# The opening of a fused transformer kernel's first stage: who clears and rotates the keys, and where the modulation products run

## The chip, the cores and the metric

One core of a Trainium2 chip runs the whole program. The metric is the device time of one execution in microseconds (us).

## The reference

Two adaptive-layernorm transformer layers over an input of 4 sequences x 512 tokens x 256 features, float32. Only the first layer's attention and the modulation vectors matter here.

```
mod = silu(c) @ wmod                 # per layer: 6 vectors of 256 for each sequence
h   = layernorm(x) * (1 + scale) + shift
q, k, v = h @ wq, h @ wk, h @ wv     # in float16; 16 query heads, 4 key groups, 16 numbers a head
q, k = rope(rmsnorm(q)), rope(rmsnorm(k))
x   = x + gate * (causal_softmax(q k^T) v @ wo)      # then a small gated feed-forward
```

The second layer is a lightning attention with a mixture of experts behind it. It needs its own modulation vectors, and 16 decay masks (one for each head), which the first stage makes and stores to memory.

## The kernel before

The program has three stages with a barrier behind each: `front_stage` (the first layer), `attention1_stage` and `experts_stage`. The change touches the first alone.

`front_order` writes out one list of events, and each engine walks through that list in order and executes the events that belong to it. TensorE (PE) works on a ring of four PSUM slots of two banks: the m-th event of the ring may start only when event m-4 has been read out. So a late reader blocks PE, and a PE event that is early in the list holds up all behind it.

Work goes by sequence b (4) and by key group g (4), 16 groups in all. For each group the events `s` (eight, by token tile and pair of heads) make the scores whose row maxima VectorE takes (L930); at the last one VectorE writes the shift into the queries (L934), `q2` turns the shifted queries, `st` makes the transposed scores, ScalarE takes their exponential (L779), GpSimd masks them (L1079), and `pv` multiplies by v. The scores of group g+1 are interleaved with the `st` of group g.

The opening, ahead of group 0, is written out by hand:

- `L stats`, `L rstd`, `L norm`: statistics of the tokens on VectorE (L174, L177), the root on GpSimd (L184 to L191), the normalization on ScalarE (L198); `xt` turns the result on PE (L206) and ScalarE applies shift and scale from `mod` (L212).
- `mod`: the modulation products, four events (L580); `mod copy` (VectorE, L852 to L843) copies them out, adds 1 to the scales (L857), and after events 1 and 3 prepares the gates.
- `pj`: q, k and v of two token tiles each on PE (L602, L604), copied out by ScalarE (L749). `sq`, `ss`, `std`, `rms`, `qn` are the RMS norm: square (L513), sum (L887), root (L757, ScalarE, which needs another activation table than the exponential), reciprocal (L890), product (L898).
- `rot`, `rope`: all 16 query heads rotated on VectorE (L907 to L921). `krot`: the 4 key heads on GpSimd (L1062 to L1073).
- `kt`: the keys turned on PE (L610) and copied out (L765); SyncE (SP) then issues 16 DMAs (L552), four for each group, that spread them over the cleared buffer `kt`. GpSimd clears that buffer (L1037) after its root of `L rstd`; VectorE clears the query buffer `qa` (L871) after `L stats`.
- `qt`: the queries of one group turned (L621) and copied out (L768).
- `dec`: one decay mask each: exponential on ScalarE (L703), triangle mask on GpSimd (L1017), store by SP (L542).

SP issues the loads of all four `x` blocks and all weights first, then walks the list too.

Of the kernel before, what the change touches and what calls it, by code (L numbers as in the profile page):

```python
# [6 lines left out]
F32 = mybir.dt.float32  # L7
# [93 lines left out]
def front_order():  # L101
# [281 lines left out]
def front_stage(nc, t, d):  # L383
# [9 lines left out]
    x, hp = t["x"], t["h_parts"]  # L393
    NH, hd, SLOTS = H0 + G0, D0 // 2, 4
    with ExitStack() as ctx:
        n = Names(nc, ctx, "front")
# [53 lines left out]
        diag = hp[:, :, :, (B - 1) * S:B * S]  # L450
        wmod1 = (qt2[:, :, :].rearrange("p g n -> p (g n)").bitcast(F32).rearrange("p (k n) -> p k n", k=KT),
                 upd[:, :, :].rearrange("p t n -> p (t n)").rearrange("p (k n) -> p k n", k=KT), ht[:, :, :])
# [28 lines left out]
        a_high, a_low, b_high, b_low = (n.sem(s) for s in ("a_high", "a_low", "b_high", "b_low"))  # L481
        carried = n.sem("carried")
        gbias_ready, x_biased, ff_done, x_done = (n.sem(s) for s in ("gbias_ready", "x_biased", "ff_done", "x_done"))
# [19 lines left out]
        MODS = ((0, (0, 1)), (0, (2, 3, 4, 5)), (1, (0, 1, 2)), (1, (3, 4, 5)))  # L503

        def rows(b):
            return slice(b * TB, (b + 1) * TB)

# [7 lines left out]
        with nc.Block() as block:  # L515

            @block.sync
            def _(sp):
# [14 lines left out]
                sp.dma_start(wo32, d["wo0"]).then_inc(wo_loaded, 16)  # L533
                for b in (2, 3):
                    sp.dma_start(x[:, rows(b), :], d["x"][:, rows(b), :]).then_inc(x_loaded[b], 16)
# [25 lines left out]
            def _(pe):  # L561
                for ev in order:
# [49 lines left out]
                    elif kind in ("qt", "q2"):  # L612
                        o = banks16(ev)
                        if kind == "qt":
                            b, g = ev[1], ev[2]
                            pe.wait_ge(q_roped, b + 1)
# [75 lines left out]
            def _(act):  # L692
# [4 lines left out]
                for ev in order:  # L697
# [45 lines left out]
                    elif kind == "pj":  # L743
                        _, b, i = ev
                        filled(act, ev)
                        if b:
                            act.wait_ge(v_copied, b)
                            act.wait_ge(qn_done, b)
                        nc.scalar.copy(qkv[:, 2 * i:2 * i + 2, :], banks(ev)[:, :, 0:QKV0]).then_inc(qkv_done, 1)  # L749
# [58 lines left out]
            def _(dve):  # L808
# [7 lines left out]
                dve.wait_ge(cond_step, 2)  # L816
                nc.vector.tensor_tensor(scond[:, :, :, :], cond[:, :, :, :], scond[:, :, :, :], ALU.mult).then_inc(scond_ready, 1)
                dve.wait_ge(slope_loaded, 16)
                nc.vector.tensor_scalar(nslope[:, :], nslope[:, :], -1.0, None, ALU.mult).then_inc(slope_neg, 1)
                gates = 0  # L820

                def gate_then(ins):
                    nonlocal gates
                    gates += 1
                    ins.then_inc(gate_step, 1)
                    dve.wait_ge(gate_step, gates)

                def columns(l):
# [17 lines left out]
                for ev in order:  # L846
# [20 lines left out]
                    elif kind == "L stats":  # L867
                        dve.wait_ge(x_loaded[ev[1]], 16)
                        norm_l.vector_stats(nc, dve, ev[1])
                        if ev[1] == 0:  # L870
                            nc.vector.memset(qa[:, :, :, :, :].rearrange("p a t h c -> p (a t h c)").bitcast(F32), 0.0  # L871
                                             ).then_inc(padding_set, 1)
                    elif kind == "A stats":
# [5 lines left out]
                    elif ev == ("sq", 0):  # L879
                        dve.wait_ge(qkv_done, 2)  # L880
                        squares(nc.vector)
                    elif kind == "ss":
                        b = ev[1]
                        dve.wait_ge(sq_done, b + 1)
                        if b:
                            dve.wait_ge(qn_done, b)
                        nc.vector.tensor_reduce(ss[:, :, :], sq[:, :, :, :], AX.X, ALU.add).then_inc(ss_done, 1)  # L887
# [3 lines left out]
                    elif kind == "qn":  # L891
                        b = ev[1]
                        dve.wait_ge(rrms_done, b + 1)
                        if b:
                            dve.wait_ge(krot_done, 2 * b)
                        else:
                            dve.wait_ge(qkv_done, 2)
                        nc.vector.tensor_tensor(qn[:, :, :, :].rearrange("p t h c -> p (t h) c"),  # L898
                                                qkv[:, :, 0:NH * D0].rearrange("p t (h c) -> p t h c", c=D0),
                                                ss[:, :, :].unsqueeze(3).to_broadcast([P, TB, NH, D0]),  # L900
                                                ALU.mult).then_inc(qn_done, 1)
                    elif kind == "rot":
                        b, q4 = ev[1], [P, TB, H0, D0]
                        dve.wait_ge(qn_done, b + 1)
                        if b == 0:
                            dve.wait_ge(tables_ready, 2)
                        nc.vector.tensor_tensor(rc_[:, :, 0:H0, :], qn[:, :, 0:H0, :],  # L907
# [3 lines left out]
                    elif kind == "rope":  # L911
                        b = ev[1]
                        q = qa[:, b % 2]
                        dve.wait_ge(rot_done, b + 1)
                        if b == 0:
                            dve.wait_ge(padding_set, 1)
                        if b >= 2:
# [57 lines left out]
            def _(pool):  # L975
# [35 lines left out]
                for ev in order:  # L1011
# [19 lines left out]
                    elif kind == "L rstd":  # L1031
                        norm_l.pool_rstd(nc, pool, ev[1])
                        if ev[1] == 0:
                            pool.wait_ge(ka_set, 1)
                            nc.gpsimd.memset(ka[:, :, :, :, D0:D0 + 1], SHIFT).then_inc(ka_set, 1)
                            tables()
                            nc.gpsimd.memset(kt[:, :, :, :].rearrange("p g r n -> p (g r n)").bitcast(F32), 0.0  # L1037
                                             ).then_inc(kt_zeroed, 1)
                    elif kind == "A rstd":
# [3 lines left out]
                    elif kind == "va":  # L1043
                        b = ev[1]
                        pool.wait_ge(qkv_done, 2 * b + 2)
                        if b >= 2:
                            pool.wait_ge(ao_done, (b - 1) * 2 * G0)
                        nc.gpsimd.tensor_copy(va[:, b % 2, :, :, 0:D0], qkv[:, :, NH * D0:QKV0].rearrange(
                            "p t (g c) -> p t g c", c=D0)).then_inc(v_copied, 1)
                    elif kind == "sq" and ev[1]:  # L1050
                        b = ev[1]
                        pool.wait_ge(qkv_done, 2 * b + 2)
                        pool.wait_ge(q_roped, b)
                        pool.wait_ge(k_roped, 2 * b)
                        squares(nc.gpsimd)
                    elif kind == "krot":
                        b, k4 = ev[1], [P, TB, G0, D0]
                        own = ka[:, b % 2, :, :, :]
                        pool.wait_ge(qn_done, b + 1)
                        if b == 0:  # L1060
                            pool.wait_ge(tables_ready, 2)
                        nc.gpsimd.tensor_tensor(rc_[:, :, H0:NH, :], qn[:, :, H0:NH, :],  # L1062
# [3 lines left out]
                        pool.wait_ge(krot_done, 2 * b + 2)  # L1066
                        if b == 0:
                            pool.wait_ge(ka_set, 2)
                        if b >= 2:
# [1853 lines left out]
```

## Time and profile before

| | |
|---|---|
| median of 3 runs | 1197.83 us (1195.2 to 1200.0) |
| the profiled execution | 1201.84 us, its span 1199.9 us |
| VectorE / PE / ScalarE busy over the span | 76% / 90% / 61% |
| first stage ends, second begins | about 270.6 us from the span's start |

A span is counted from the first to the last instruction of the profiled execution. All times of rows are counted from its start. A timeline row gives the start, the duration, the engine, the line, what is written and read, and in brackets the idle time ahead of it with what ended it. "PE" rows are matmuls, "PEld" rows weight loads.

### The profile page before, as it was taken

How to read it: one execution, taken by the hardware profiler on the slowest of the kernel's cores; microseconds unless marked ns; L12 is line 12 of the kernel's file. 1: busy time of each engine (PE TensorE's matmuls, PEld its weight loads, DVE VectorE, ACT ScalarE, POOL GpSimd, SP SyncE). 2: the span in 40 equal slices, each digit the busy share in tenths (PEclk: the TensorE clock that was granted, in tenths of full speed). 3: DMA queues.
4: the chain of work that ended last, by engine and by line, in shares of the span. 5: the costliest groups of instructions: out<-in, count | busy, mean ns of one | idle time of the engine just before them, and what ended most of it. 6: DMA issues, size and time to landing. Idle time of an engine off the chain costs nothing. (4 is left out here: it accounts for less than half of the span.)

```text
span 1199.9 us, 21640 instructions
## 1 busy us (share of the span) xinstructions
PE 1075.4 (90%) x7276; PEld 920.5 (77%) x7276; DVE 915.4 (76%) x1832; ACT 735.0 (61%) x1389; POOL 351.7 (29%) x358
## 2 busy tenths in 40 slices
PE   5778787868899999999999999999999987869995
PEld 5545555546788998899989998899989976658993
DVE  5687979856778878778778788787787776867765
ACT  5477686766667566566666666666666653625650
POOL 5365545344411111101110111101111333843440
PEclk9699897988999999999999999999999996979997
DMA  8110000109503004003003003003000001443436
GB/s 305 28 45 19 7 14 12 43 2 100 116 1 125 10 2 123 9 9 115 9 9 115 9 9 115 9 25 98 9 18 27 1 1 51 146 142 105 121 92 214
DMA packets 62325, 72.16 MB, mean 60 GB/s; under 512 B 21841, under 2 KB 49617, under 8 KB 61234
## 3 DMA queue, kind: packets, MB, share of 16 engines
q1 hardware_dynamic: 58850, 61.90, 19.1%
q0 software_dynamic: 3408, 9.39, 2.1%
q8 instruction: 39, 0.64, 0.2%
q14 instruction: 28, 0.23, 0.1%
HBM read 36.39 MB, written 32.78 MB: 58 GB/s over the span
## 5 line engine op out<-in xcount | busy, mean ns | idle before, releaser
L1396 PE MATMUL attn_psum<-all_h_parts,attn_wp 128*128 128x512 f32 x1152 | 301.5, 397 | 0.0
L1396 PEld LDWEIGHTS attn_psum<-all_h_parts,attn_wp 128*128 128x128 f32 x1152 | 211.6, 189 | 40.9
L1551 ACT CAST attn_pp<-attn_p 128x512 fp32r<-128x512 f32 (+3 forms) x256 | 117.3, 458 | 198.7 <-DVE attn_p L1645 196.7
L1776 POOL TENSOR_TENSOR all_gate<-all_gate,attn_sq 128x512 f32<-128x512 f32 x64 | 84.6, 1322 | 502.0 <-ACT attn_sq L1562 501.9
L1626 DVE TENSOR_TENSOR attn_pp<-attn_p,attn_pp 128x512 fp32r<-128x512 f32 (+3 forms) x256 | 198.5, 775 | 8.1 <-ACT attn_pp L1551 8.1
L1475 PE MATMUL attn_psum<-attn_qkp 128*128 128x512 f32 (+3 forms) x768 | 164.4, 323 | 4.1 <-DVE attn_qkp L1626 4.1
L1422 PE MATMUL attn_psum<-attn_pp,attn_vp 128*128 128x512 f32 (+3 forms) x768 | 162.9, 321 | 0.8 <-issue 0.5
L1422 PEld LDWEIGHTS attn_psum<-attn_pp,attn_vp 128*128 128x128 f32 x768 | 129.0, 189 | 21.2 <-issue 1.4
L1475 PEld LDWEIGHTS attn_psum<-attn_qkp 128*128 128x128 f32 x768 | 125.1, 189 | 12.7 <-issue 4.6
L930 DVE TENSOR_REDUCE front_top<-front_psum 128x2 f32<-128x256 f32 (+3 forms) x128 | 100.7, 816 | 34.1 <-PE front_psum L636 34.0
L1645 DVE TENSOR_TENSOR attn_p<-attn_psum,attn_mask 128x512 f32<-128x512 f32 (+3 forms) x256 | 123.5, 483 | 3.3 <-PE attn_psum L1475 2.1
L1406 PE MATMUL attn_psum<-all_wop,attn_yp 128*128 128x256 f32 x768 | 102.6, 285 | 7.3 <-DVE attn_yp L1626 7.3
L1626 DVE TENSOR_TENSOR attn_yp<-attn_y,attn_yp 128x512 fp32r<-128x512 f32 x64 | 45.6, 713 | 79.7 <-ACT attn_yp L1559 79.7
L779 ACT ACTIVATE front_probs<-front_psum 128x1024 f16<-128x1024 f32 (+3 forms) x128 | 83.9, 705 | 34.8 <-PE front_psum L643 34.6
L1406 PEld LDWEIGHTS attn_psum<-all_wop,attn_yp 128*128 128x128 f32 x768 | 97.1, 194 | 7.6 <-DVE attn_yp L1626 7.6
L1391 PE MATMUL attn_psum<-attn_wp,all_h_parts 128*128 128x256 f32 x768 | 101.2, 281 | 0.0
L1626 DVE TENSOR_TENSOR attn_qkp<-attn_qk,attn_qkp 128x512 fp32r<-128x512 f32 x128 | 88.2, 689 | 10.5 <-ACT attn_qkp L1526 10.3
L1391 PEld LDWEIGHTS attn_psum<-attn_wp,all_h_parts 128*128 128x128 f32 x768 | 95.3, 188 | 0.0
L1526 ACT CAST attn_qkp<-attn_qk 128x512 fp32r<-128x512 f32 x128 | 79.4, 621 | 4.1
L1523 ACT ACTIVATE attn_qk<-attn_psum 128x512 f32<-128x512 f32 x128 | 75.8, 593 | 4.8 <-PE attn_psum L1396 4.7
L643 PE MATMUL front_psum<-front_qt,front_kt 128*128 128x512 f16 (+3 forms) x256 | 58.7, 343 | 21.0 <-ACT front_probs L779 8.7
L1626 DVE TENSOR_TENSOR attn_vp<-attn_v,attn_vp 128x512 fp32r<-128x512 f32 x64 | 44.3, 692 | 32.8 <-ACT attn_vp L1544 32.8
(358 smaller groups left out, 1841.6 us busy)
## 6 DMA issues: line engine op xcount, KB each, us to landing
expert_rows<-attn_empty SPq DMA_DIRECT2D x8, 2080.0 KB, 10.2
all_wraw<-in_w1p SPq DMA_DIRECT2D x8, 1024.0 KB, 5.2
all_yacc<-expert_rows SPq DMA_DIRECT2D x39, 130.5 KB
attn_mask<-decay_masks SPq DMA_DIRECT2D x16, 256.0 KB, 2.6
experts_wx<-expert_results SPq DMA_DIRECT2D x6, 512.0 KB, 8.4
experts_xraw<-in_wx SPq DMA_DIRECT2D x4, 608.0 KB
all_wraw<-in_wx SPq DMA_DIRECT2D x4, 608.0 KB
all_x<-in_x SPq DMA_DIRECT2D x4, 512.0 KB, 10.8
```

Of the source, the lines that this page charges most:

```text
L779: nc.scalar.activation(probs[:, pr, j, :, 0:S - j * P], banks(ev)[:, :, 0:S - j * P], ACT.Exp, scale=D0 ** -0.5).then_inc(exp_done, 1)
L930: nc.vector.tensor_reduce(top[:, tt, h:h + 2], banks(ev)[:, :, 0:(tt + 1) * P], AX.X, ALU.max).then_inc(top_done, 1)
L1391: last = nc.tensor.matmul(out[:, i * 2 * P:(i + 1) * 2 * P], hh[:, a, k, tt * P:(tt + 1) * P], wp[:, c, k, col:col + 2 * P], start=(m == 0 ...
L1396: last = nc.tensor.matmul(out, wp[:, a, k, col:col + P], hh[:, c, k, b * S:(b + 1) * S], start=(m == 0), stop=(m == 5))
L1406: last = nc.tensor.matmul(ps[:, Y_BANK + i, half * D:(half + 1) * D], yp[:, a, h, tt * P:(tt + 1) * P], wop[:, c, h, :], start=(m == 0), s ...
L1422: last = nc.tensor.matmul(ps[:, O_BANK + h, j * P:S], vp[:, b % 2, a, j, h * P:(h + 1) * P], pp[:, h, c, OFF[j]:OFF[j] + S - j * P], start ...
L1475: last = nc.tensor.matmul(bank(task)[:, 0:S - j * P], qkp[:, h, a, 1, j * P:(j + 1) * P], qkp[:, h, c, 0, j * P:S], start=(m3 == 0), stop= ...
L1526: nc.scalar.copy(qkp[:, (unit + 1) % 2, 0, which, :], qk[:, which, :]).then_inc(hi_sem, 1)
L1551: nc.scalar.copy(pp[:, u % 2, 0, cols], p[:, cols]).then_inc(p_hi, 1)
L1626: nc.vector.tensor_tensor(out, whole, high.bitcast(F32), ALU.subtract).then_inc(ready, 1)
L1645: nc.vector.tensor_tensor(p[:, cols], bank(task)[:, 0:S - j * P], mask[:, u % 2, 0:S - j * P], ALU.mult).then_inc(p_masked, 1)
L1776: nc.gpsimd.tensor_tensor(cols, cols, sq[:, h, :], ALU.add).then_inc(summed, 1)
```

## The change

- The list: `L stats` and `L rstd` come ahead of all decay events; only 8 decays (not 10) come before the keys' DMAs in SP's walk, decays 8 and 9 after group 0's scores.
- The clearing of `qa` moves to VectorE's idle time ahead of `L stats`; the clearing of `kt` moves from GpSimd to VectorE, behind `L stats`.
- The square and the sum of sequence 0 go by halves of two token tiles, each behind its own half of `pj`.
- For sequence 0 the norm product and rotation of the keys run on VectorE, ahead of the queries'; the queries follow in three pieces (`rp` 0: group 0, `rp` 1: group 1, `rp` 2: groups 2 and 3), the last behind the first score event.
- GpSimd's copy of v (`va`, L1048) waits until the keys are rotated.
- `mod` 2 moves behind `qt` of group 0, `mod` 3 behind all of group 0's scores. One third of the second layer's modulation weights is loaded into the last `x` block's buffer instead of `qt2`'s, so the load of that block waits until all four `mod` events are copied; SP issues it ahead of sequence 1's key DMAs.

```diff
-    order = (decays(0, 4) + [("L stats", 0), ("L rstd", 0)] + decays(4, 8) + [("mod", 0), ("mod copy", 0), ("L norm", 0),
-             ("cast",), ("xt", 0)] + decays(8, 10) + [("pj", 0, 0), ("pj", 0, 1), ("mod", 1), ("mod", 2), ("va", 0), ("sq", 0),
-             ("ss", 0), ("std", 0), ("rms", 0), ("qn", 0), ("rot", 0), ("krot", 0), ("rope", 0), ("kt", 0), ("qt", 0, 0),
-             ("mod copy", 1), ("mod copy", 2), ("mod", 3)] + scores(0)[:2] + [("mod copy", 3)] + scores(0)[2:])
+    order = ([("L stats", 0), ("L rstd", 0)] + decays(0, 5) + [("mod", 0), ("mod copy", 0), ("L norm", 0), ("cast",),
+             ("xt", 0)] + decays(5, 7) + [("pj", 0, 0)] + decays(7, 8) + [("pj", 0, 1), ("mod", 1), ("sq", 0), ("std", 0),
+             ("rms", 0), ("krot", 0), ("kt", 0), ("rp", 0), ("qt", 0, 0), ("mod", 2), ("mod copy", 1), ("va", 0),
+             ("rp", 1), ("mod copy", 2)] + scores(0)[:2] + [("rp", 2)] + scores(0)[2:] + [("mod", 3)] + decays(8, 10)
+             + [("mod copy", 3)])
...
                     elif ev[0] == "kt":
                         b = ev[1]
+                        if b == 1:
+                            sp.wait_ge(mod_copied, 4)
+                            sp.dma_start(x[:, rows(B - 1), :], d["x"][:, rows(B - 1), :]).then_inc(x_loaded[B - 1], 16)
                         sp.wait_ge(kt_done, b + 1)
...
                     elif kind == "q2":
                         filled(act, ev)
-                        if ev[1] == 0:
-                            act.wait_ge(mod_copied, 4)
...
                         if ev[1] == 0:
-                            nc.vector.memset(qa[:, :, :, :, :].rearrange("p a t h c -> p (a t h c)").bitcast(F32), 0.0
-                                             ).then_inc(padding_set, 1)
+                            nc.vector.memset(kt[:, :, :, :].rearrange("p g r n -> p (g r n)").bitcast(F32), 0.0
+                                             ).then_inc(kt_zeroed, 1)
...
                     elif ev == ("sq", 0):
-                        dve.wait_ge(qkv_done, 2)
-                        squares(nc.vector)
+                        for i in range(2):
+                            tiles = slice(2 * i, 2 * i + 2)
+                            qk = qkv[:, tiles, 0:NH * D0]
+                            dve.wait_ge(qkv_done, i + 1)
+                            nc.vector.tensor_tensor(sq[:, tiles, :, :].rearrange("p t h c -> p t (h c)"), qk, qk, ALU.mult
+                                                    ).then_inc(half_squared, 1)
+                            dve.wait_ge(half_squared, i + 1)
+                            last = nc.vector.tensor_reduce(ss[:, tiles, :], sq[:, tiles, :, :], AX.X, ALU.add)
+                        last.then_inc(ss_done, 1)
...
+                    elif kind == "rp":
+                        i = ev[1]
+                        heads = slice(R0 * i, H0 if i == 2 else R0 * (i + 1))
+                        q, q4 = qa[:, 0, :, heads, :], [P, TB, heads.stop - heads.start, D0]
+                        first_normed(heads, i + 2)
+                        nc.vector.tensor_tensor(rc_[:, :, heads, :], qn[:, :, heads, :],
+                                                cos_t[:, :, 0, :].unsqueeze(2).to_broadcast(q4), ALU.mult)
+                        nc.vector.tensor_tensor(rs_[:, :, heads, :], qn[:, :, heads, :],
+                                                sin_t[:, :, 0, :].unsqueeze(2).to_broadcast(q4), ALU.mult).then_inc(g_turned, 1)
+                        dve.wait_ge(g_turned, i + 1)
...
                         b = ev[1]
                         pool.wait_ge(qkv_done, 2 * b + 2)
+                        if b == 0:
+                            pool.wait_ge(k_roped, 2)
```

`first_normed` is the norm product of the heads given, one instruction; `krot` of sequence 0 is the same five instructions (product, two rotations, subtract, add) on 4 heads, on VectorE.

## Rows read from the trace of the kernel before

**Rows 1.** The page: the span of the profiled execution.
```profile
span 1199.9 us, 21640 instructions
```
**Rows 2.** Timeline, 7 to 18 us: from the statistics to the modulated tokens.
```profile
7.74 0.38 DVE L177 BATCH_NORM_AGGREGATE front_l_mv<-front_l_st 128x2 f32<-128x6 f32 x4
...
8.49 1.76 DVE L871 MEMSET front_qa<- 128x2048 f32 x1 [0.38 <-issue]
8.51 0.29 POOL L1017 TENSOR_SCALAR_AFFINE_SELECT all_wraw<-all_wraw 128x128 f32<-128x128 f32 x1 [0.32 <-ACT all_wraw L703]
...
8.96 2.54 ACT L703 ACTIVATE all_yacc<-front_dist,front_nslope 128x512 f32<-128x512 f32 x4
...
9.51 0.24 POOL L184 TENSOR_SCALAR front_l_rstd<-front_l_mv 128x4 f32<-128x4 f32 x1
...
11.45 2.07 ACT L198 ACTIVATE all_yacc<-all_x,front_l_shift,front_l_rstd 128x256 f32<-128x256 f32 x4
...
12.64 3.78 DVE L857 TENSOR_SCALAR all_mod<-all_mod 128x8 f32<-128x8 f32 x1
...
12.88 3.51 POOL L1037 MEMSET front_kt<- 128x4096 f32 x1
...
13.66 1.94 PE L206 MATMUL front_psum<-all_ident,all_yacc 128*128 128x128 f32 x8 [1.27 <-ACT all_yacc L198]
...
16.52 1.45 ACT L212 ACTIVATE front_ht<-front_psum,all_mod 128x512 f16<-128x512 f32 x2 [1.65 <-DVE all_mod L857]
```
**Rows 3.** Timeline, 21 to 36 us: from the projections to the keys' DMAs.
```profile
21.83 4.08 PE L580 MATMUL front_psum<-front_scond,front_wmod 128*128 128x4 f32 x32
22.08 0.80 ACT L749 CAST front_qkv<-front_psum 128x768 f16<-128x768 f32 x1 [1.12 <-PE front_psum L604]
...
22.91 1.49 DVE L513 TENSOR_TENSOR front_rope_cos<-front_qkv 128x1280 f32<-128x1280 f16 x1 [6.49 <-ACT front_qkv L749]
...
26.41 0.65 DVE L890 RECIPROCAL front_ss<-front_ss 128x80 f32<-128x80 f32 x1 [0.49 <-ACT front_ss L757]
...
32.92 0.89 POOL L1073 TENSOR_TENSOR front_ka<-front_rope_cos,front_rope_sin 128x128 f16<-128x128 f32 x1
...
35.19 10.24 SPq L552 DMA_DIRECT2D front_kt<-front_kall  x16
```
**Rows 4.** Timeline, 36 to 54 us: group 0's scores and what follows them.
```profile
36.43 3.55 PE L580 MATMUL front_psum<-front_scond,front_ht 128*128 128x4 f32 x16
...
40.90 0.42 DVE L930 TENSOR_REDUCE front_top<-front_psum 128x2 f32<-128x256 f32 x1 [5.62 <-PE front_psum L636]
...
42.67 5.60 DVE L930 TENSOR_REDUCE front_top<-front_psum 128x2 f32<-128x256 f32 x7
```
**Rows 5.** Timeline, 44 to 75 us: the first exponentials and the next scores.
```profile
48.39 1.53 DVE L174 BATCH_NORM_STATS2 front_l_st<-all_x 128x6 f32<-128x256 f32 x4
48.62 0.46 PEld L621 LDWEIGHTS front_psum<-all_ident,front_qa 128*128 128x128 f16 x8 [3.69 <-DVE front_top L930]
...
49.68 1.28 ACT L703 ACT_TABLE_LOAD   x1
...
50.97 0.72 ACT L703 ACTIVATE all_wraw<-front_dist,front_nslope 128x512 f32<-128x512 f32 x1
...
53.72 0.69 DVE L930 TENSOR_REDUCE front_top<-front_psum 128x2 f32<-128x512 f32 x1 [2.75 <-PE front_psum L636]
```
**Rows 6.** Windows: length, busy us of each engine, granted clock, DMA share, GB/s.
```profile
28.00:30.00 2.00, 2.00 (x11) 2.00 (x11) 1.97 (x3) 0.00 (x0) 1.33 (x1) 0.50 0.29 110
...
42.00:44.00 2.00, 2.00 (x16) 1.40 (x15) 1.90 (x7) 0.00 (x0) 0.00 (x0) 0.69 0.21 49
...
50.00:60.00 10.00, 8.16 (x46) 4.84 (x44) 6.13 (x12) 9.66 (x16) 7.04 (x9) 0.66 0.08 29
```
**Rows 7.** Source L920: min/median/max ns of one; source L552: issue to landing.
```profile
L920 DVE TENSOR_TENSOR front_qa<-front_rope_cos,front_rope_sin x4: 679/826/1095, 31.5 to 202.7; 128x512 f16<-128x512 f32 x4
...
DMA to landing us min/median/max: 1.8/1.9/2.1
```

More of the change, by code:

```diff
@@ L394, in front_stage, with rows @@
     NH, hd, SLOTS = H0 + G0, D0 // 2, 4
+    def rows(b):
+        return slice(b * TB, (b + 1) * TB)
     with ExitStack() as ctx:
@@ L450, in front_stage @@
         diag = hp[:, :, :, (B - 1) * S:B * S]
[L451 removed]
+        wmod1 = (x[:, rows(B - 1), :].rearrange("p (k t) n -> p k (t n)", k=KT),
                  upd[:, :, :].rearrange("p t n -> p (t n)").rearrange("p (k n) -> p k n", k=KT), ht[:, :, :])
@@ L533, in _ @@
                 sp.dma_start(wo32, d["wo0"]).then_inc(wo_loaded, 16)
-                for b in (2, 3):
-                    sp.dma_start(x[:, rows(b), :], d["x"][:, rows(b), :]).then_inc(x_loaded[b], 16)
+                sp.dma_start(x[:, rows(2), :], d["x"][:, rows(2), :]).then_inc(x_loaded[2], 16)
                 sp.dma_start(wffn32, d["wffn"]).then_inc(ffn_loaded, 16)
@@ L826, in gate_then, with first_normed @@
                     dve.wait_ge(gate_step, gates)
+                def first_normed(heads, count):
+                    width = heads.stop - heads.start
+                    if count == 1:
+                        dve.wait_ge(rrms_done, 1)
+                    nc.vector.tensor_tensor(qn[:, :, heads, :],
+                                            qkv[:, :, heads.start * D0:heads.stop * D0].rearrange(
+                                                "p t (h c) -> p t h c", c=D0),
+                                            ss[:, :, heads].unsqueeze(3).to_broadcast([P, TB, width, D0]),
+                                            ALU.mult).then_inc(g_normed, 1)
+                    dve.wait_ge(g_normed, count)
                 def columns(l):
@@ L901, in _ @@
                                                 ALU.mult).then_inc(qn_done, 1)
+                    elif ev == ("krot", 0):
+                        k4, own = [P, TB, G0, D0], ka[:, 0, :, :, :]
+                        first_normed(slice(H0, NH), 1)
+                        dve.wait_ge(tables_ready, 2)
+                        nc.vector.tensor_tensor(rc_[:, :, H0:NH, :], qn[:, :, H0:NH, :],
+                                                cos_t[:, :, 1, :].unsqueeze(2).to_broadcast(k4), ALU.mult).then_inc(krot_done, 1)
+                        nc.vector.tensor_tensor(rs_[:, :, H0:NH, :], qn[:, :, H0:NH, :],
+                                                sin_t[:, :, 1, :].unsqueeze(2).to_broadcast(k4), ALU.mult).then_inc(krot_done, 1)
+                        dve.wait_ge(krot_done, 2)
+                        dve.wait_ge(ka_set, 2)
+                        nc.vector.tensor_tensor(own[:, :, :, 0:hd], rc_[:, :, H0:NH, 0:hd], rs_[:, :, H0:NH, hd:D0],
+                                                ALU.subtract).then_inc(k_roped, 1)
+                        nc.vector.tensor_tensor(own[:, :, :, hd:D0], rc_[:, :, H0:NH, hd:D0], rs_[:, :, H0:NH, 0:hd],
+                                                ALU.add).then_inc(k_roped, 1)
+                    elif kind == "rp":
[8 more added lines that the diff above has]
+                        dve.wait_ge(g_turned, i + 1)
+                        if i == 0:
+                            dve.wait_ge(padding_set, 1)
+                        nc.vector.tensor_tensor(q[:, :, :, 0:hd], rc_[:, :, heads, 0:hd], rs_[:, :, heads, hd:D0], ALU.subtract)
+                        last = nc.vector.tensor_tensor(q[:, :, :, hd:D0], rc_[:, :, heads, hd:D0], rs_[:, :, heads, 0:hd],
+                                                       ALU.add)
+                        last.then_inc(g_roped, 1)
@@ L1052, in _ @@
                         pool.wait_ge(qkv_done, 2 * b + 2)
-                        pool.wait_ge(q_roped, b)
+                        pool.wait_ge(g_roped, 3)
+                        if b > 1:
+                            pool.wait_ge(q_roped, b - 1)
                         pool.wait_ge(k_roped, 2 * b)
                         squares(nc.gpsimd)
-                    elif kind == "krot":
+                    elif kind == "krot" and ev[1]:
                         b, k4 = ev[1], [P, TB, G0, D0]
                         own = ka[:, b % 2, :, :, :]
-                        pool.wait_ge(qn_done, b + 1)
-                        if b == 0:
-                            pool.wait_ge(tables_ready, 2)
+                        pool.wait_ge(qn_done, b)
                         nc.gpsimd.tensor_tensor(rc_[:, :, H0:NH, :], qn[:, :, H0:NH, :],
```

40 lines of the change are left out of this document (18 added, 22 removed).

## Prediction

> **What bounds the kernel now.** I read the page first: span 1199.9 us [rows 1]. The profiled execution took 1201.84 us, 1.94 more than its span and 4.0 more than the median of the runs. The sum below is a difference, made on the profiled execution and then taken from the median. The change touches only the first stage, about 270 us long, and there only the opening, so the timeline of the first 60 us was the view to read, engine by engine, for what ends each wait.
>
> *Up to the modulated tokens* [rows 2]: the statistics are done at 8.12 (L177), but GpSimd starts on the root at 9.51, after decay masks; ScalarE normalizes from 11.45, 1.94 later, when its eight decays (to 11.50) are through as well. PE has turned the tokens at 15.60; ScalarE still waits 1.65 us, for L857: an addition on 8 columns that lasts 3.78 us and ends just after GpSimd's clearing of `kt` (12.88 to 16.39). The tokens are ready at 17.97.
>
> *Up to the keys* [rows 3]: square, sum, root, reciprocal, product of all 20 heads, and GpSimd's rotation of the keys end at 33.81; the key DMAs are issued from 35.19, one each 0.64 us (10.24 / 16).
>
> *The scores* [rows 3, 4]: four DMAs issued from 35.19 on serve group 0; the fourth starts at 37.1 and lands at most 2.1 later [rows 7], at 39.2. But PE stands in `mod` 3 until 39.98, and the first reduction starts at 40.90. So the modulation product is the last wait, by 0.8 us. Then `mod copy` 3 (41.32 to 42.67), seven reductions to 48.27, and the turned shifted queries at 48.6.
>
> *Behind that* [rows 5, 6]: ScalarE must reload the exponential's table (1.28 us) ahead of decay 10. PE and VectorE wait for it: VectorE idles 2.75 us before the reduction at 53.72. From 50 to 60 us ScalarE is busy 9.66 of 10. After that the order is a fixed interleave in which each engine waits for the others in turn, so I take it that what the opening gives is passed on.
>
> **The change part by part.**
>
> *Statistics first, five decays.* The root starts at 8.2 instead of 9.51, and the normalization can follow 1.94 later, at 10.15. Five decays at 0.64 (2.54 / 4) end at 9.7. The normalization runs 10.15 to 12.2 and the turning (1.94) to 14.3, with ScalarE's weight casts beside it.
>
> *The clearings.* That of `qa` falls into VectorE's wait for the slope load: nothing. That of `kt` costs VectorE 2 x 1.76 = 3.5 us, from 8.5 to 12.0 [rows 2], ahead of `mod copy` 0, which isn't due before 12.4 (L857 behind it began at 12.64): nothing as well. If it were slower, up to 1.8 us are hidden by the turning. Without GpSimd's clearing L857 takes some 0.2 us. The tokens are ready at 14.35 + 1.45 = 15.8, 2.2 us earlier.
>
> The row says more: L857 seems to have stood still while GpSimd wrote. The Trainium skill (SBUF — State Buffer, section "SBUF: two separate sides") says that VectorE and GpSimd share a pair of SBUF ports under an exclusive lock, held for a whole instruction by whoever comes first. It speaks against this change: VectorE's clearing would shut GpSimd out of the root. Under VectorE's clearing of `qa` (8.49 to 10.25) GpSimd started a mask at 8.51 and took 0.29 for it, and began the root at 9.51 [rows 2]; here the trace doesn't bear the rule out. By the rule the root would start at 12.0, by the rows at 8.2. It is rival 3.
>
> *Halves.* The projections take 4.1 us from ready tokens to the second copy (17.97 to 22.08), so the copies start at 18.0 and 19.9 and end at 18.8 and 20.7 [rows 3]. An elementwise VectorE instruction of 1280 columns takes 1.49 and one of 512 takes 0.68 [rows 3, 7]: 0.14 + 1.06 for each 1000. A half (640) is then 0.81, and I take the same for its sum. The second half ends at 20.75 + 1.65 = 22.4, against 25.9 (22.91 plus twice 1.49): 3.5 earlier. The root's table load (1.28) is done by 22.2. Root and reciprocal end 1.14 later, as before: 23.55.
>
> *Keys first, on VectorE.* Three instructions of 256 columns at 0.41 and two of 128 at 0.27, with 0.1 for waits: 1.9, to 25.4 instead of 33.81, 8.4 earlier. Two bounds: 1.5 if the gaps overlap, 3 if small strided pieces run at half speed. The key DMAs start 1.4 later, at 26.8; the fourth starts at 28.7 and lands at 30.8. From 28 to 30 us DMA was nearly free (share 0.29) [rows 6]; 1 MB less (two decays, one `x` block) stands ahead of the keys now, so it should be clear by then. Even a queue full until 29 gives 31.1, not the last wait.
>
> *`rp` 0 and `mod` 2.* `rp` 0 costs the same 1.9, to 27.3 (GpSimd's copy of v beside it may add 0.5), the turning ends at 27.9. `mod` 1, four vectors, is 32 matmul instructions [rows 3], so `mod` 2 with three is 24. The sixteen of [rows 4] took 0.222 each at the lower level, 1.2 GHz; the 32 of `mod` 1 took 0.128: 5.3 or 3.1 us. The granted clock was 0.50 from 28 us on and came back only within 42 to 44 (0.69) [rows 6]: it fell while PE was busy with such four-column products. PE now does the same and idles more, so I take 5.3: PE is free at 33.3. This is the last wait again; `rp` 1 and `mod copy` 1 (1.9 + 1.4) are done at 30.6. The first reduction came 0.92 after the products; now at 34.2, **6.7 us earlier**.
>
> *What is given back.* `rp` 2, eight heads: 3 x 0.68 + 2 x 0.41 + 0.1 = 2.95, now between the first reduction and the other seven. It runs 34.65 to 37.6, the seven end at 43.2. `mod` 3 may start when the fifth of all reductions has freed its slot, about 40.0, and takes 3.1 (to 43.1) or 5.3 (to 45.3). The scores were what brought the clock back, some 3 us after they began [rows 4, 6]; they begin at 33.4 now, so I lean to 3.1. The shifted queries turn at 43.6 (45.4) against 48.62: **5.0 (3.2) earlier**. `mod copy` 3 (1.4) and the statistics of sequence 1 (1.9) come now between them and group 1's scores: 46.7 (48.7) against 50.3.
>
> *The table load.* Decays 8 and 9 carry it into ScalarE's wait during the scores (from 35 us): 1.28 off ScalarE's chain. In the trace the next activation starts 0.01 behind the load [rows 5]. The Trainium skill (ScalarE: Activation LUTs, section "What ACT_TABLE_LOAD costs") gives 1.28 and a drain of 1.38 for each switch; by it 1.4 more would be gained here, and the trace shows no such drain. With it ScalarE alone would be 6.3 (4.5) ahead, but VectorE isn't: group 1's third score needs a slot that is read at 47.1 (49.1), so its reduction comes at about 48.6 (50.6) instead of 53.72, 5.1 (3.1) earlier.
>
> *The rest.* The late `x` block: SP issues it before sequence 1's key DMAs, tens of us ahead of its reader; one issue of 0.6 us: nothing. Sequences 1 to 3 keep their work.
>
> Sum: 5.1 or 3.1, mostly the first: 4.5 us. 1199.9 becomes 1195.4, the profiled time 1197.3, the median 1197.83 - 4.5 = **1193.3 us**.
>
> **The rivals.**
>
> 1. *The clock stays up in `mod` 2 as well.* 2.2 us more before the scores, still behind the keys' landing (30.8 against 31.1). Against it: the lower clock by 28 us, under the same kind of work. Gain 7.3, and up to 8 with both good bounds: 1190.
> 2. *Absorbed.* The opening is ahead, but the lead is lost in the interleave, as half-clock stretches fall elsewhere. From 50 to 60 us the granted clock was 0.66 [rows 6]; a stretch more of about 6 us in which PE is busy 80% and takes twice as long costs up to 2.5. With the half-clock case of `mod` 3, 3.1 - 2.5 leaves 0.6: 1197.2.
> 3. *The lock.* GpSimd's root waits for VectorE's clearing and starts at 12.0. The normalization is then at 14.0 instead of 11.45 and the tokens at 19.5, 1.5 later than before; everything behind shifts by 3.7 from my forecast, so 4.5 becomes 0.8, and with `mod` 3 at half clock (2 less) the kernel is 1.2 slower: 1199. From a root start of 12.7 on it decides the sign alone. For it the 3.78 of L857, against it the mask at 8.51.
>
> **How the numbers follow.** A measurement of this kernel tells about 0.5%, 6.0 us, from no change; nearly all of my cases lie within it. Forecast 0.60 at 1193.3 (own range 1190.5 to 1196); rival 1 0.14 at 1190; rival 2 0.18 at 1197.2; rival 3 0.08 at 1199. Faster by over 0.5% means under 1191.8: most of rival 1 and a fifth of the forecast, 0.26. Slower by over 0.5% needs the lock and two more half-clock stretches, or something I don't see: 0.07. The same: 0.67. The range goes from 1188.8, a little beyond rival 1, to 1199.8, rival 3 and the scatter of the median.
>
> **What would show it.** L857 at 0.2 us and the tokens ready near 15.8; the keys rotated near 25.4; first key DMA near 26.8; first score reduction near 34.2; the shifted queries turned at 43.6 (45.4 if `mod` 3 is at half clock); no table load between `q2` and decay 10; second stage beginning near 266. It would be wrong if GpSimd's root starts at 12, if the small rotations cost twice as much, if the granted clock differs over more than 5 us from before behind 50 us, or if the lead at 54 us isn't there at 260.

## The result, and the profile after

| | before | after |
|---|---|---|
| median, 20 runs each | 1198.69 us (1195.02 to 1202.89) | 1195.16 us (1191.16 to 1200.06) |
| ratio | 1 | 0.9969, 95% interval 0.9958 to 0.998 |
| the profiled execution's span | 1199.9 us | 1191.2 us |
| its second stage begins at | 270.6 us | 262.5 us |

The ratio is 3.7 us (2.4 to 5.0) of 1198.7: a small gain, but one whose interval leaves out zero. The forecast was 4.5, at 1193.3 us; the median fell at 1195.16, inside its range and inside the half per cent that the prediction counts as the same. The two profiled executions lie 8.7 apart: 1201.84 us is 3.2 above the median before, and the profiled execution after, 1193.11 us, is 2.1 below its own.

The timeline after, 7 to 16 us, answers to [rows 2]:

```profile
7.65 0.38 DVE L178 BATCH_NORM_AGGREGATE front_l_mv<-front_l_st 128x2 f32<-128x6 f32 x4
...
8.21 0.23 POOL L185 TENSOR_SCALAR front_l_rstd<-front_l_mv 128x4 f32<-128x4 f32 x1 [2.43 <-DVE front_l_mv L178]
...
8.72 1.04 POOL L188 TENSOR_TENSOR front_l_rstd<-front_l_rstd,all_neg_half 128x4 f32<-128x4 f32 x1
...
8.83 3.47 DVE L893 MEMSET front_kt<- 128x4096 f32 x1 [0.80 <-issue]
...
9.91 0.20 POOL L192 TENSOR_TENSOR front_l_shift<-front_l_shift,front_l_rstd 128x4 f32<-128x4 f32 x1
...
10.14 2.08 ACT L199 ACTIVATE all_yacc<-all_x,front_l_shift,front_l_rstd 128x256 f32<-128x256 f32 x4 [0.55 <-POOL front_l_shift L192]
...
12.56 0.17 DVE L879 TENSOR_SCALAR all_mod<-all_mod 128x8 f32<-128x8 f32 x1
...
14.34 1.45 ACT L213 ACTIVATE front_ht<-front_psum,all_mod 128x512 f16<-128x512 f32 x2 [0.78 <-PE front_psum L207]
```

The clearing of `kt` takes VectorE 3.47 us where GpSimd took 3.51, GpSimd finishes the root beside it, and the addition (now L879) takes 0.17 instead of 3.78. ScalarE now waits for PE's turning, no longer for VectorE.

The same timeline from 17 to 46 us, answering to [rows 3 to 5]:

```profile
19.65 3.75 PE L585 MATMUL front_psum<-front_scond,front_wmod 128*128 128x4 f32 x32
...
19.90 0.80 ACT L759 CAST front_qkv<-front_psum 128x768 f16<-128x768 f32 x1 [0.50 <-PE front_psum L609]
...
22.90 0.65 DVE L920 RECIPROCAL front_ss<-front_ss 128x80 f32<-128x80 f32 x1 [0.49 <-ACT front_ss L767]
...
25.05 0.29 DVE L941 TENSOR_TENSOR front_ka<-front_rope_cos,front_rope_sin 128x128 f16<-128x128 f32 x1
...
26.72 10.93 SPq L557 DMA_DIRECT2D front_kt<-front_kall  x16
...
27.21 0.59 PE L629 MATMUL front_psum<-all_ident,front_qa 128*128 128x128 f16 x4 [1.15 <-DVE front_qa L956]
...
30.97 1.85 PE L585 MATMUL front_psum<-front_scond,front_upd 128*128 128x4 f32 x8
...
32.86 0.18 DVE L874 COPY all_mod<-front_psum 128x24 f32<-128x24 f32 x1 [2.69 <-PE front_psum L585]
...
33.73 0.42 DVE L983 TENSOR_REDUCE front_top<-front_psum 128x2 f32<-128x256 f32 x1 [0.48 <-PE front_psum L644]
33.91 1.28 ACT L711 ACT_TABLE_LOAD   x1
...
36.82 5.60 DVE L983 TENSOR_REDUCE front_top<-front_psum 128x2 f32<-128x256 f32 x7
...
40.26 1.93 PE L585 MATMUL front_psum<-front_scond,front_ht 128*128 128x4 f32 x16
42.45 0.20 DVE L987 TENSOR_SCALAR front_qa<-front_top 128x16 f16<-128x16 f32 x1
```

The first reduction stands at 33.73 instead of 40.90, 7.2 us earlier. Before, the last wait ahead of it was for product 3; now it is for product 2, which ends at 32.82. The table load lies in ScalarE's wait. Group 0's shift stands at 42.45; in the profile before it was at 48.30.

Two marks of the later progress (moments that every execution of either kernel has) were read from the timelines of all executions: VectorE's shift (one instruction for each of the 16 groups) and the first instruction of the second stage. The table has them for every profiled execution; "rest" is the span from there to the end, of which the change touches nothing.

| execution | first reduction | shift, group 0 | shift, group 1 | second stage | rest |
|---|---|---|---|---|---|
| before | 40.90 | 48.30 | 60.54 | 270.61 | 929.3 |
| before_again | 39.76 | 47.16 | 58.81 | 268.31 | 932.3 |
| after | 33.73 | 42.45 | 54.03 | 262.53 | 928.7 |
| after_again | 33.68 | 42.40 | 55.91 | 265.81 | 932.9 |
| after_third | 33.53 | 42.25 | 53.07 | 261.85 | 930.9 |
| clear_only | 39.44 | 46.84 | 58.28 | 268.06 | 930.9 |
| keys_on_gpsimd | 33.73 | 42.45 | 54.03 | 262.57 | 931.1 |
| products_back | 35.75 | 45.90 | 56.54 | 265.43 | 930.2 |
| table_back | 34.42 | 43.12 | 57.30 | 266.30 | 931.8 |
| halves_back | 35.22 | 43.94 | 54.73 | 264.53 | 931.9 |
| queries_whole | 38.07 | 44.50 | 55.03 | 264.33 | 931.9 |
| rp2_early | 33.37 | 40.05 | 50.74 | 260.44 | 932.0 |
| rp2_early_again | 33.79 | 40.21 | 50.74 | 259.79 | 930.0 |
| rp2_early_mod3_late | 32.73 | 39.39 | 49.42 | 262.80 | 931.7 |

### The profile page after: what moved, and what is told of

Its sections match the earlier page's. It is cut to its first block and busy times, and to the rows that moved or that the text cites. A ratio compares the mean times of both kernels' runs of the same rounds, so it can differ in the third digit from the quotient of the medians.

```text
span 1191.2 us, 21657 instructions
## 1 busy us (share of the span) xinstructions
PE 1073.6 (90%) x7276; PEld 919.8 (77%) x7276; DVE 916.4 (77%) x1850; ACT 735.7 (62%) x1389; POOL 343.3 (29%) x353
```

## The experiments

**The two kernels again.** No edit. They ask how far one execution is from another, and whether the lead of the opening is passed on to the second stage.

> The kernel before once more, to see how far one execution differs from another. If the lead of the opening (6.5 us at group 1, 8.1 at the second stage) is passed on, the shifts of the 16 groups fall within 0.5 us of 48.3, 60.5, ... 253.5 and the second stage begins at 270.6, and the scatter of the times is made behind the first stage. If the first stage itself scatters, as clock stretches fall elsewhere, the second stage begins anywhere from 267 to 274.

> The changed kernel once more. If the lead is made once and passed on: shift of group 0 at 42.5, of group 1 at 54.0, second stage at 262 to 264, and a ratio near 0.9945 (6.5 of 1198). If half of it is lost on average, as the medians say (3.5 us), the second stage begins at 265 to 267 in this execution and the ratio stays near 0.997.

> The changed kernel a third time, on one chip with rp2_early_again. Group 0's shift at 42.4; group 1's at 54.0 if product 3 runs at full clock, at 55.9 if at half; the second stage at 262.5 or 265.8 with it. Ratio 0.995 to 0.998.

Measured: ratios 1.0006 (0.9991 to 1.0022), 0.9955 (0.9938 to 0.9973) and 0.9963 (0.9949 to 0.9977). The rest of the program takes 928.7 to 932.9 us, and its mean is 930.8 over the two executions before and 930.8 over the three after: the scatter of the times is made there as much as in the first stage, and not by the change. The lead at group 1 (6.5 us in the first pair) is 6.8 at group 10 and 8.1 at the second stage, so it is passed on. Why it changes by 1.6 on the way isn't shown; the stretches at half clock fall at other moments in each execution.

The first pair flatters the change. The kernel before did not come back to 270.6 us, the first case expected of its repeat: its second stage began at 268.31, and its first reduction came 1.14 us earlier. The tokens were 0.58 earlier there (L212 at 15.94, not 16.52), and the projections, whose last matmuls ran at the higher clock, took 0.56 less. Over the two executions before and the three after, the mean lead is 6.7 us at the first reduction, 5.3 at group 1 and 6.1 at the second stage.

And after_again loses 1.9 us between two marks, with the same start. Its timeline shows where:

```profile
40.20 1.81 PE L585 MATMUL front_psum<-front_scond,front_upd 128*128 128x4 f32 x8
41.87 3.55 PE L585 MATMUL front_psum<-front_scond,front_ht 128*128 128x4 f32 x16
42.40 0.20 DVE L987 TENSOR_SCALAR front_qa<-front_top 128x16 f16<-128x16 f32 x1
45.28 1.01 PE L629 MATMUL front_psum<-all_ident,front_qa 128*128 128x128 f16 x8
45.46 0.18 DVE L874 COPY all_mod<-front_psum 128x24 f32<-128x24 f32 x1 [2.86 <-PE front_psum L585]
```

The last 16 instructions of product 3 take 3.55 us there and 1.93 in the profile above: the half-clock and the full-clock case of the prediction, each in an execution of the same kernel. The product ends at 45.42 and 42.19 (predicted 45.3 and 43.1). after_third, with product 3 at full clock, has group 1's shift at 53.07, 1.0 ahead of the 54.0 expected.

**clear_only**: the two clearings in the kernel before.

```diff
+                nc.vector.memset(qa[...], 0.0).then_inc(padding_set, 1)
                 dve.wait_ge(slope_loaded, 16)
...
-                            nc.vector.memset(qa[...], 0.0).then_inc(padding_set, 1)
+                            nc.vector.memset(kt[...], 0.0).then_inc(kt_zeroed, 1)
...
-                            nc.gpsimd.memset(kt[...], 0.0).then_inc(kt_zeroed, 1)
```

> The kernel before with the two clearings alone moved: query buffer into VectorE's wait for the slope, key buffer from GpSimd to VectorE behind the statistics. If VectorE's clearing doesn't shut GpSimd out and GpSimd's clearing did hold L857: the root starts at 9.5 as before, L857 takes 0.2 us instead of 3.8, the modulated tokens begin at 15.7 instead of 16.5 (0.8 earlier), and the first key DMA as well; but modulation product 3 still ends near 39.5, so group 0's shift comes no more than 0.5 us earlier. If the lock works both ways, the root starts at 12.0 and the tokens begin near 18.

Measured: ratio 0.9979 (0.9965 to 0.9994).

```profile
8.32 3.47 DVE L873 MEMSET front_kt<- 128x4096 f32 x1 [0.80 <-issue]
...
8.93 0.23 POOL L184 TENSOR_SCALAR front_l_rstd<-front_l_mv 128x4 f32<-128x4 f32 x1
9.44 1.04 POOL L187 TENSOR_TENSOR front_l_rstd<-front_l_rstd,all_neg_half 128x4 f32<-128x4 f32 x1
...
12.42 0.21 DVE L859 TENSOR_SCALAR all_mod<-all_mod 128x8 f32<-128x8 f32 x1
15.06 1.45 ACT L212 ACTIVATE front_ht<-front_psum,all_mod 128x512 f16<-128x512 f32 x2 [0.78 <-PE front_psum L206]
```

The root begins at 8.93 under VectorE's clearing, and L859 takes 0.21 us. So GpSimd's clearing did hold VectorE's addition, and VectorE's does not hold GpSimd: the lock of rival 3 isn't there for a clearing on VectorE. Against before_again, whose root also began at 8.93, the tokens begin 0.88 us earlier (15.94 there) and the first reduction 0.32. The missing 0.56 isn't a wait for the products: it is lost already at the projections' second copy (20.62 against 20.94), as the last projections ran at the lower clock here (0.85 us for two matmuls) and at the higher in before_again (0.49). Against before, whose projections ran at the lower clock too and whose root began 0.58 later, group 0's shift comes 1.46 earlier, so the clearing alone is worth 0.9 at a like clock. The timed gain, 2.5 us (0.7 to 4.2), is more than either; this stays open.

**keys_on_gpsimd**: the keys' four rotation instructions on GpSimd again, the norm product of the keys still first on VectorE.

```diff
                     elif ev == ("krot", 0):
                         first_normed(slice(H0, NH), 1)
-                        nc.vector.tensor_tensor(rc_[:, :, H0:NH, :], ...)      # and the three behind it
...
-                    elif kind == "krot" and ev[1]:
+                    elif kind == "krot":                                       # GpSimd, behind g_normed 1
```

> The changed kernel with the keys of sequence 0 rotated on GpSimd again, still ahead of the queries. If VectorE's rotation is worth its place: four instructions of 0.73 to 1.76 us instead of 1.5 us in all, the keys rotated at 27.5 to 30 instead of 25.3, and since PE turns them ahead of the queries and of product 2, everything behind shifts by 2.5 to 4.5: shift of group 0 at 45 to 47. If product 2 would be the last wait anyway, 42.5 as in the changed kernel.

Measured: ratio 0.9946 (0.9931 to 0.9962). Its first case, a shift of group 0 at 45 to 47, was wrong; the second (42.5) came.

```profile
24.70 0.90 POOL L1111 TENSOR_TENSOR front_rope_sin<-front_qn,front_sin_t 128x256 f32<-128x256 f32 x1
...
26.15 0.49 POOL L1118 TENSOR_TENSOR front_ka<-front_rope_cos,front_rope_sin 128x128 f16<-128x128 f32 x1
26.26 0.53 DVE L945 TENSOR_TENSOR front_qa<-front_rope_cos,front_rope_sin 128x128 f16<-128x128 f32 x1
...
26.79 0.58 PE L615 MATMUL front_psum<-all_ident,front_ka 128*128 128x128 f16 x4 [3.56 <-POOL front_ka L1118]
...
27.59 3.52 PE L585 MATMUL front_psum<-front_scond,all_x 128*128 128x4 f32 x16
28.02 10.74 SPq L557 DMA_DIRECT2D front_kt<-front_kall  x16
```

The keys are rotated at 26.64 instead of 25.34 and their DMAs start 1.3 us later (28.02, 26.72), and nothing behind it moves: product 2 begins at 27.59 in both, and the marks agree to 0.1 us up to the second stage. In the changed kernel PE, with the keys turned, stands 1.15 us for the first queries (L629), so that wait is the one that counts there. Here PE waits for the keys (L615) and turns the queries right behind them: GpSimd's 1.3 us just fill that slack, and a slower rotation would show. VectorE has the queries at 26.79 here and at 27.06 in the changed kernel: freed of the keys, it gains only 0.3, as its two rotation products take 0.83 and 0.94 us beside GpSimd's, not 0.50 and 0.41. after_again says the same of the keys: PE turned them 0.8 us late, behind a product 1 at half clock, and the first reduction did not move. The two intervals of the changed kernel and of this one overlap; no gain of one over the other is shown.

**halves_back** and **queries_whole**: the other two parts of VectorE's chain, one undone in each.

```diff
-                        for i in range(2):
-                            tiles = slice(2 * i, 2 * i + 2)
+                        for i in range(1):                    # halves_back
+                            tiles = slice(0, TB)
...
-                                pe.wait_ge(g_roped, min(g, 2) + 1)
+                                pe.wait_ge(g_roped, 3)        # queries_whole; rp 1, rp 2 ahead of qt 0
```

> The changed kernel with square and sum of sequence 0 whole, behind the second copy. Two instructions of 1.49 behind the copy instead of 1.65: the norm, the first queries, product 2 and the first reduction all 1.4 us later (35.1), group 0's shift at 43.8. If PE's clock decides instead, product 2 ends where it did and the shift stays at 42.4.

> The changed kernel with all three pieces of the query rotation ahead of group 0's queries' turning, still with product 2 behind it. Pieces 1 and 2 (1.75 and 2.75 us) then stand ahead of the turning, product 2 and the scores: first reduction at 38.2 instead of 33.7; nothing is given back behind it, so the reductions end 5.6 + 0.4 later, at 44.3, and group 0's shift is 1.8 us later than in the changed kernel, 4.1 later than in rp2_early. If the turning isn't in the path, 40.1 as in rp2_early.

Measured in one execution each (1198.4 and 1198.18 us, which alone tell nothing), with product 3 at full clock in both. Halves undone: first reduction 35.22, shift 43.94, 1.5 later than in the changed kernel; second stage 2.0 later. The queries whole: first reduction 38.07 (38.2 was expected), 4.3 later, and shift 44.50, 2.0 later; second stage 1.8 later. Both terms are in the path in full up to the first reduction, and half of the second comes back, since `rp` 2 no longer stands between the reductions.

**products_back**: products 2 and 3 in their old places.

```diff
-... ("pj", 0, 1), ("mod", 1), ("sq", 0), ... ("qt", 0, 0), ("mod", 2), ("mod copy", 1), ...
+... ("pj", 0, 1), ("mod", 1), ("mod", 2), ("sq", 0), ... ("qt", 0, 0), ("mod copy", 1), ...
...
-             ("rp", 1), ("mod copy", 2)] + scores(0)[:2] + [("rp", 2)] + scores(0)[2:] + [("mod", 3)] + ...
+             ("rp", 1), ("mod copy", 2), ("mod", 3)] + scores(0)[:2] + [("rp", 2), ("mod copy", 3)] + scores(0)[2:] + ...
```

> The changed kernel with the modulation products 2 and 3 where they were: 2 right behind 1, ahead of the keys' turning, 3 ahead of group 0's scores, its copy behind the third piece of the query rotation. If the products' place is what made the lead (keys_on_gpsimd showed that the keys are not the last wait): PE ends product 2 at 27 to 29 and turns the keys 1.5 to 3 us late, product 3 ends at 34.5 to 35.5, group 0's first reduction comes at 35.5 to 36.5 instead of 33.7, and group 0's shift at 45.5 to 46.5 instead of 42.4; without the copy behind it group 1's shift is at 55.5 to 57. If the products cost little wherever they stand: first reduction 33.7 to 34.5.

Measured: ratio 0.9997 (0.9979 to 1.0016), no gain left in the times. The keys wait for product 2 (DMAs from 30.04 instead of 26.72), the first reduction comes at 35.75, the shifts at 45.90 and 56.54, all as expected; the second stage begins 2.9 later than after, 2.9 earlier than before_again. By the marks the products' place is worth some 3 us (2.0 against the mean of the changed kernel) and 3 are left to the rest of the change. The times show less left: at most 2.5 us. Three of the ten runs lie at 1203 to 1204 us and the other seven at 1195.4 to 1200.7; why isn't shown. Products 2 and 3 moved together here, so their shares aren't told apart.

**table_back**: decays 8 and 9 ahead of the second projection's copy.

```diff
-... + [("pj", 0, 0)] + decays(7, 8) + [("pj", 0, 1), ...
+... + [("pj", 0, 0)] + decays(7, 10) + [("pj", 0, 1), ...
```

> The changed kernel with decays 8 and 9 ahead of the second projection's copy, so that the exponential's table is loaded behind the first shifted queries again, ahead of decay 10. The projection's copy comes 0.7 to 0.8 us later (two activations of 0.66, less the wait), and so does group 0's shift (43.2). If the load is hidden by VectorE (gates and statistics end at 45.8, the load ends 1.3 us later than the activation did): group 1's shift 0.8 to 1.4 us later than 54.0. If the load counts in full: 2.0 later, 56.0. All of it read against an execution with product 3 at the same clock.

Measured: ratio 0.9987 (0.9974 to 1.0001). Product 3 ran at half clock, so after_again is its match: group 0's shift 0.72 later, group 1's 1.39, of which the load is 0.67; the second stage 0.5 later. About half of the 1.28 us is hidden. The times show more lost: 1.6 us are left of the gain, against 3.7 to 5.4 in the three comparisons of the changed kernel.

**rp2_early** and its repeat: the third piece into VectorE's wait for product 2 (2.69 us in the timeline after, ahead of L874).

```diff
-             ("rp", 1), ("mod copy", 2)] + scores(0)[:2] + [("rp", 2)] + scores(0)[2:] + [("mod", 3)] + ...
+             ("rp", 1), ("rp", 2), ("mod copy", 2)] + scores(0) + [("mod", 3)] + ...
```

> The changed kernel with the third piece of the query rotation (2.75 us on VectorE) moved from behind the first score reduction to behind the second piece, where VectorE waited 2.7 us for product 2. If that wait is free: first reduction still at 33.7, group 0's reductions end at 39.7 and its shift comes 2.7 us earlier, at 39.7; product 3 starts near 36.5 and ends at 39.5 (full clock) or 41.8 (half), and group 1's shift comes 2 to 2.7 us earlier than in the changed kernel at the same clock. A ratio 0.002 lower than the changed kernel's. If product 3 at half clock becomes the last wait in most executions, 1 us or less is left.

> The kernel of rp2_early again. Group 0's shift at 40.0 to 40.5; group 1's at 50.7 with product 3 at full clock, and at 53.5 to 54.5 with it at half (it would end at 42.7 and take what was won). If the 2 us of its first profile hold on average, its ratio is 0.001 to 0.002 below the changed kernel's of this call; if product 3 runs at half clock in most executions, the two are alike.

Measured: ratios 0.9961 (0.9943 to 0.9978) and 0.9954 (0.9939 to 0.9968). In both profiles the first reduction stays where it was within 0.4 us, group 0's shift comes 2.4 and 2.2 earlier and the second stage 2.1 and 2.7 earlier than in the first profile of the changed kernel, at a like clock in product 3 (1.93 us for its last 16 in both). In the times it is not told from the changed kernel (0.9963 for after_third, against the same runs of the kernel before as the repeat). By the traces it is the best version; by the times it beats the kernel before, no more.

**rp2_early_mod3_late**: rp2_early, and product 3 and its copy moved on, out of the opening's list and into the interleave of group 1.

```diff
-FIRST_AT = {"dec10": (0, 0), ...
+FIRST_AT = {"mod3": (1, 2), "modc3": (1, 5), "dec10": (0, 0), ...
```

> As rp2_early, and product 3 with its copy and gates (1.4 us of VectorE) moved into the interleave of group 1. If product 3 stands in the path at half clock: group 0's shift at 39.7 and the shifted queries turned 0.4 behind it in every execution, group 1's shift near 50.5 whatever the clock, 3.5 us earlier than the changed kernel's better case, of which product 3 then takes back 1 to 2 within group 2: second stage 3 to 5 us earlier than in the changed kernel at a like clock, ratio 0.990 to 0.993. If PE is as short of time in the interleave: all of it comes back, and it ends with rp2_early.

Measured: ratio 0.9979 (0.9967 to 0.9991). The shift of group 1 is at 49.42, 4.6 earlier than after, but at group 2 only 1.5 are left, and the second stage begins no earlier than after (262.80), 2.4 and 3.0 us later than in the two executions of rp2_early. Neither case of the expectation came.

```profile
53.65 0.95 PE L586 MATMUL front_psum<-front_scond,front_upd 128*128 128x4 f32 x8
...
54.46 1.93 PE L586 MATMUL front_psum<-front_scond,front_ht 128*128 128x4 f32 x16
...
56.66 0.42 DVE L984 TENSOR_REDUCE front_top<-front_psum 128x2 f32<-128x256 f32 x1 [3.61 <-PE front_psum L645]
...
57.09 1.73 ACT L788 ACTIVATE front_probs<-front_psum 128x1024 f16<-128x1024 f32 x2 [2.45 <-PE front_psum L652]
```

The product takes PE 2.7 us (53.65 to 56.39) even at full clock, and VectorE (3.61) and ScalarE (2.45) both stand idle for it; at the same places of rp2_early VectorE waits 1.01 and ScalarE not at all. In the interleave no wait of PE hides it. Behind group 0's scores one does: in the timeline after, the product runs from 39.35 to 42.19 while VectorE is still at the reductions (to 42.42).

## Why the prediction was right

*The sum.* 4.5 us forecast, 3.7 measured, with 5.4 and 4.4 in the two repeats. On the marks the first stage is 6.1 us shorter (mean of 269.5 over two executions against 263.4 over three), some 1.5 more than the times say; with a rest that scatters by 4 us that difference can't be settled here. So the mechanism is borne out mark by mark, while the closeness of 3.7 to 4.5 is in part luck: the second stage was forecast near 266 and began at 262.5, 265.8 and 261.9.

*Step by step.* The clearing, the root, the halves and the small rotations came out as priced: tokens ready at 15.8 (15.8 predicted), keys rotated at 25.34 (25.4), first key DMA at 26.72 (26.8), PE free of product 2 at 32.82 (33.3), first reduction at 33.73 (34.2), the seven reductions' end at 42.42 (43.2), the shifted queries at 42.8 (43.6). Small terms were each a little too dear: `rp` 2 took 2.8 and not 2.95, and it began 0.6 earlier. Group 1's third score came at 47.01 (48.6), 1.6 before its forecast, so the lead there was 6.7 and not 5.1. Against the repeat of the kernel before, where it came at 52.15, the lead is 5.1.

*The clock.* The forecast leaned to product 3 at full clock with half clock as its other case. Both came, and the ends were 0.1 to 0.9 us from the predicted ones. In four executions of the changed kernel or one with the same marks (after, after_again, after_third, keys_on_gpsimd) it was half once. A sign named for being wrong came too, and it was a bad one: from 50 to 60 us the granted clock was 0.66 before and 0.97 after, but 0.95 in before_again, the kernel before once more. It tells two executions apart, not two kernels.

*What was credited to the wrong part.* "Keys first, on VectorE ... 8.4 earlier" is right as a time, but only 1.3 of it comes from the engine, and none of that reaches the scores (keys_on_gpsimd); what counts is that the first queries are ready early, as product 2 stands behind them. The working said that the keys' landing was not the last wait, and the sum went by product 2, so the total didn't suffer. By the marks, products_back shows the products' place at 2 to 3 us, queries_whole the queries in pieces at 2, halves_back the halves at 1.5 to 2, table_back the load at 0.7 of 1.28 at group 1 (0.5 with the decays' place at the second stage), clear_only the clearing at 0.9 (0.3 where the clock took the rest). Each rests on one execution, and the times of clear_only, products_back and table_back don't agree with the marks. The statistics ahead of all decays were never undone alone, nor was the late `x` block.

*The give-back.* "`rp` 2 ... now between the first reduction and the other seven" was found, but I didn't ask whether VectorE had a place for it: it waited 2.69 us just before. rp2_early shows that the give-back was avoidable.

*The rivals.* Rival 1 (product 2 at full clock) was seen in no execution. Rival 2's stretches do fall elsewhere in each execution, but the lead isn't absorbed: its mean is 5.3 us at group 1 and 6.1 at the second stage. Rival 3 is refuted for this clearing: in clear_only it starts at 8.32 and GpSimd's root at 8.93, and in the changed kernel the root is through at 10.11 while it runs to 12.30. The Trainium skill (SBUF — State Buffer, section "SBUF: two separate sides") ties the lock, on VectorE's side, to an operation in a two-port mode or with two inputs in SBUF. The prediction left that condition out, so its "by the rule the root would start at 12.0" is more than the page says. The traces fit the condition: VectorE's clearing, which reads nothing, left GpSimd's root at its old durations (1.04 us for L188 beside it), while GpSimd's own clearing held an addition of 8 columns for 3.78 us.

## What to carry to other kernels

When several chains lead to one instruction, price a speed-up only on the one that arrives last, and test it by handing the other chains their old cost back: here the most visible edit, the keys' new engine, was worth nothing, as PE had a slack of 1.15 us for it. Work that must go somewhere goes into a wait that the trace shows, and the wait's engine and length have to fit: product 3, moved from behind group 0's scores into the filled interleave, cost 2.4 to 3.0 us more. After placing it, look once more for idle time just ahead of what was pushed back. And take the profile of the old kernel twice: of the 6.5 us between the first two, 1.7 lay between two executions of the old kernel itself.

## What the hardware showed unexpectedly

*A clock column that misses a fall.* The window view of after_again gives a granted clock of 1.00 from 40 to 46 us, while the source view of the same execution gives every weight load of product 3 333 ns, the duration at 1.2 GHz (192 ns at 2.4, the value of all sixteen in after):

```profile
40.00:46.00 6.00, 6.00 (x35) 6.00 (x34) 3.07 (x10) 0.09 (x1) 0.00 (x0) 1.00 0.14 54
```

```profile
L585 PEld LDWEIGHTS front_psum<-front_scond,front_ht x16: 333/333/333, 41.8 to 45.0; 128*128 128x128 f32 x16
```

It isn't alone: in after_again, clear_only, table_back and rp2_early_again the column reads 1.00 from 26 to 34 us, and in the other ten profiles 0.54 or less from 26 to 28 us and 0.50 from 28 to 34, while the median weight load of product 2's first sixteen takes 333 ns in all fourteen. In the opening of this kernel the level is read from durations.

*One kernel, two courses.* PE stood at the lower level through product 3 in after_again and at the higher in after, with the first reduction and group 0's shift equal within 0.1 us. The clock alone makes 1.9 us at group 1. Product 1 was at the lower level too in after_again (6.83 us for its 32 instructions, 3.75 in after), but the one doesn't follow from the other: in rp2_early_again product 1 took 6.82 and the last sixteen of product 3 took 1.93.

*Short GpSimd instructions beside short VectorE ones.* Before, GpSimd's last key subtraction of 128 columns took 0.89 us [rows 3]; beside VectorE's pieces of four heads it took 0.49 (L1118), and the whole rotation by GpSimd ran from 23.8 to 26.6 instead of 28.7 to 33.8.
